# Mean and variance of every normalisation by `bn_aggr`, one per block of 128 tokens, in place of seven small operations

## The reference

```python
def _layernorm(x, axis=-1, eps=1e-05):
    m = jnp.mean(x, axis=axis, keepdims=True)
    v = jnp.var(x, axis=axis, keepdims=True)
    return (x - m) / jnp.sqrt(v + eps)
...
x = x + jnp.tanh(g_xattn[0]) * _L0_xattn_ref(_layernorm(x, axis=-1), ...)
x = x + jnp.tanh(g_ffn[0]) * _L0_ffn_ref(_layernorm(x, axis=-1), ...)
x = x + jnp.tanh(g_xattn[1]) * _L1_xattn_ref(_layernorm(x, axis=-1), ctx_1024, ctx_1024, ...)
x = x + jnp.tanh(g_ffn[1]) * _L1_ffn_ref(_layernorm(x, axis=-1), ...)
```

## Time and profile before

| what | value |
|---|---|
| median of 3 runs | 1592.85 us |
| lowest and highest run | 1590.7 and 1597.24 us |
| the profiled execution, from its first to its last instruction | 1595.5 us |
| DVE busy | 972.5 us, 61% of the span |
| PE busy | 1302.9 us, 82% |
| ACT busy | 1081.9 us, 68% |
| POOL busy | 528.5 us, 33% |
| mean granted TensorE clock | 0.920 of full speed |

### The profile page before, as it was taken

The page is one execution under the profiler, slowest core; times in us unless marked ns, Lnnn a source line. Parts: engine busy times, 40 slices in busy tenths (PEclk is TensorE's granted clock), DMA queues, the critical chain, the costliest instruction groups (busy, mean ns, idle before and its releaser), DMA issues.

```text
span 1595.5 us, 34655 instructions
## 1 busy us (share of the span) xinstructions
PE 1302.9 (82%) x11876; PEld 764.7 (48%) x11876; DVE 972.5 (61%) x2365; ACT 1081.9 (68%) x1781; POOL 528.5 (33%) x505
## 2 busy tenths in 40 slices
PE   6777776887588999998998899979997886888860
PEld 2212332343235554655475546554666575577650
DVE  7987558536743775388538854896468765223323
ACT  5998886867886799878987997769872431222220
POOL 1101121121453121425543445246425334503216
PEclk8978897988798999999999999999998997899995
DMA  7654402503132343454444554434346545579964
GB/s 225 223 188 123 105 1 67 137 4 83 69 90 73 87 121 86 103 157 140 140 113 120 148 143 113 128 102 152 100 126 192 144 132 135 164 191 236 252 174 119
DMA packets 234434, 207.60 MB, mean 130 GB/s; under 512 B 121945, under 2 KB 191137, under 8 KB 234273
## 3 DMA queue, kind: packets, MB, share of 16 engines
q1 hardware_dynamic: 210017, 160.29, 38.1%
q0 software_dynamic: 12288, 33.57, 6.6%
q10 hardware_dynamic: 11968, 11.54, 2.3%
HBM read 110.01 MB, written 70.16 MB: 113 GB/s over the span
## 4 chain that ended last, share of the span: by engine, by line
PE 48%; DVE 20%; ACT 18%; issue 7%; POOL 4%; DMA 1%; another core or an unknown queue 1%; SPq 0%; POOLq 0%; ACTq 0%; DVEq 0%
ACT tanh_tiles L1251 15%; PE psF L1020 8%; PE psE L866 6%; PE psE L868 5%; PE psE L867 5%; PE psY L866 3%; PE psY L867 2%; PE psY L868 2%; PE psF L872 2%; PE psF L866 2%; PE psF L868 2%; PE psF L867 2%; POOL work L852 2%; DVE stats L1428 2%; DVE xn L1454 1%
## 5 line engine op out<-in xcount | busy, mean ns | idle before, releaser
L1251 ACT ACTIVATE tanh_tiles<-feat,text_bias 128x512 f32<-128x512 f32 x1232 | 774.4, 713 | 74.1 <-DVE feat L1624 56.2
L1020 PE MATMUL psF<-tanh_tiles,wslide 128*32 128x512 f32 x2464 | 372.9, 662 | 61.7 <-ACT tanh_tiles L1251 60.5
L1653 DVE TENSOR_TENSOR tile<-tile,psE 128x512 f32<-128x512 f32 x128 | 87.5, 684 | 163.9 <-ACT tile L1278 80.6
L799 POOL TENSOR_TENSOR hid<-tile,hid 128x512 f16<-128x512 f32 x76 | 88.3, 1163 | 233.4 <-ACT hid L1270 231.8
L823 POOL DMA_INDIRECT xs_rows<-xs,slot_i x128 | 127.8, 998 | 111.7 <-PE psF L1020 40.3
L1270 ACT CAST hid<-tile 128x512 f16<-128x512 f32 x128 | 78.6, 614 | 125.5 <-DVE tile L1653 115.8
L866 PE MATMUL psY<-down,hid 128*128 128x256 f16 x512 | 143.3, 280 | 15.9 <-issue 10.1
L868 PE MATMUL psE<-xg,up_lo 128*128 128x128 f16 x768 | 146.8, 221 | 9.2 <-issue 9.1
L867 PE MATMUL psE<-xg,up_hi 128*128 128x128 f16 x768 | 147.3, 222 | 7.5 <-issue 7.5
L1278 ACT ACTIVATE tile<-psE 128x512 f32<-128x512 f32 x128 | 75.6, 591 | 114.7 <-remote 60.8
L866 PE MATMUL psE<-xg,up_hi 128*128 128x128 f16 x768 | 147.5, 222 | 6.7 <-issue 5.6
(11 more groups left out here) (306 smaller groups left out, 2883.9 us busy)
## 6 DMA issues: line engine op xcount, KB each, us to landing
down<-down_split SPq DMA_DIRECT2D x208, 256.0 KB
y_rows<-hid SPq DMA_DIRECT2D x52, 256.0 KB
xs_rows<-peakT SPq DMA_DIRECT2D x24, 512.0 KB, 6.4
y_rows<-tanh_tiles ACTq DMA_DIRECT2D x44, 256.0 KB
down_split<-hid SPq DMA_DIRECT2D x18, 256.0 KB, 3.2
xscan<-in_x SPq DMA_DIRECT2D x8, 512.0 KB, 5.1
x<-in_x SPq DMA_DIRECT2D x8, 512.0 KB, 5.3
w_lin<-w_split SPq DMA_DIRECT2D x15, 256.0 KB
```

The source lines that it names most:

```text
L799: pool.tensor_tensor(hid_lo[:, n], tile[:, v.n % 2], hid_hi[:, n], ALU.subtract).then_inc(glo_done, 1)
L1020: last = pe.matmul(psF[32 * j:32 * j + 32, RHO, :], wslide[:, c, 31 - g:63 - g], tanh_tiles[:, st.at(SETS, 2 * g + c) % HRING, j], start=g ...
L1251: act.activation(tanh_tiles[:, n % HRING, j], feat[:, c], ACT.Tanh, bias=text_bias[:, c, col:col + 1]).then_inc(h_ready, 1)
L1653: dve.tensor_tensor(tile[:, n], tile[:, n], psE[:, (2 * v.n + 1) % 3], ALU.mult).then_inc(g_done, 1)
```

## The change

The moments are finished by one `bn_aggr` for each block of 128 tokens, which turns the block's six columns into mean and variance and writes them to the block's column of `norm[:, 0]` and `norm[:, 1]`. The addition of EPS moves to the head of `inverse_root`, as an operation of its own, which writes `veps`. The three Newton iterations are written out in place of a loop of three; the instructions are the same.

```diff
             def moments(ch, src, norm):
 
-                mean = norm[:, 0]
                 for t in range(NT):
                     last = dve.bn_stats(stats[:, t, :], src[:, t, :])
                 ch.link(last)
-
-                dve.tensor_tensor(mean, stats[:, :, 1], stats[:, :, 4], ALU.add)
-                dve.tensor_tensor(dif[:, :], stats[:, :, 1], stats[:, :, 4], ALU.subtract)
-                ch.link(dve.tensor_tensor(veps[:, :], stats[:, :, 2], stats[:, :, 5], ALU.add))
-                dve.tensor_scalar(mean, mean, 0.5, None, ALU.mult)
-                dve.tensor_tensor(dif[:, :], dif[:, :], dif[:, :], ALU.mult)
-                ch.link(dve.tensor_scalar(veps[:, :], veps[:, :], 1.0 / D, EPS, ALU.mult, ALU.add))
-                ch.link(dve.scalar_tensor_tensor(out=veps[:, :], in0=dif[:, :], scalar=0.25, in1=veps[:, :],
-                                                 op0=ALU.mult, op1=ALU.add))
+                for t in range(NT):
+                    last = dve.bn_aggr(norm[:, :, t], stats[:, t, :])
+                ch.link(last)
 
             def inverse_root(ch, rstd):
 
+                ch.link(dve.tensor_scalar(veps[:, :], rstd, EPS, None, ALU.add))
                 ch.link(dve.tensor_scalar(rstd.bitcast(I32), veps[:, :].bitcast(I32), -0.5, 1597463007.0,
                                           ALU.mult, ALU.add))
-                for _ in range(3):
-                    ch.link(dve.tensor_tensor(nwt[:, :], rstd, rstd, ALU.mult))
...
+                ch.link(dve.tensor_tensor(nwt[:, :], rstd, rstd, ALU.mult))
...
```

More of the change, by code:

```diff
@@ new lines, in inverse_root @@
+                ch.link(dve.scalar_tensor_tensor(out=nwt[:, :], in0=nwt[:, :], scalar=-0.5, in1=veps[:, :],
+                                                 op0=ALU.mult, op1=ALU.mult))
+                ch.link(dve.scalar_tensor_tensor(out=rstd, in0=nwt[:, :], scalar=1.5, in1=rstd,
+                                                 op0=ALU.add, op1=ALU.mult))
+                ch.link(dve.tensor_tensor(nwt[:, :], rstd, rstd, ALU.mult))
+                ch.link(dve.scalar_tensor_tensor(out=nwt[:, :], in0=nwt[:, :], scalar=-0.5, in1=veps[:, :],
+                                                 op0=ALU.mult, op1=ALU.mult))
```

## The result

| | median us | runs | ratio to before (95% interval) |
|---|---|---|---|
| before | 1593.49 (1590.7 to 1597.24) | 5 | |
| changed | 1582.21 (1577.61 to 1584.59) | 5 | 0.9921 (0.9895 to 0.9948) |

The change makes the kernel 11.3 us faster, 0.8%. It was measured twice more beside the experiments, each time on a chip with its own level: 1602.99 to 1587.07, ratio 0.9892 (0.9862 to 0.9921), and 1556.52 to 1538.99, ratio 0.9881 (0.9863 to 0.9898). The intervals of the first and the third share only 0.9895 to 0.9898; the first gain is the smallest of the three.

The account below looks back on a forecast made before the run. No single engine bounds the chain (PE 48%, DVE 20%, ACT 18%); DVE counts at boundaries, standing behind POOL. 7.2 + 2.2 + 1.2 = 10.6 us off 1592.85 gives 1582.3, range 1573 to 1592.

Parts of the forecast that it names:

- The aggregation: In each norm, four bn_aggr replace seven DVE operations: 0.47 us in place of 0.89, never held by POOL.
- (a): Rival at the boundaries: POOL holds the aggregation as well; only 2.4 us gained, 1590 us; chance 0.10.
- (c): Rival in every norm: the aggregation is as long as bn_stats or longer; 1593 us, no change, or slower; chance 0.10.
- The head of the root: Start of inverse_root in each norm: the added linked tensor_scalar costs 0.20 us; no wait for POOL charged.
- A late boundary: Last four of six outer-step ends, where LN4 and scan norm meet: 1.8 us gained each, 7.2 us together.
- An early boundary: First two of six outer-step ends: 1.0 us gained at the first, 1.2 at the second, 2.2 us together.
- Six other norms: Norms on the chain away from the boundaries: each 0.2 us shorter, 1.2 us together.
- (b): Rival at the boundaries: half of the gain is absorbed where three engines meet; 1588 us; chance 0.20.
- (d): Rival at up to five boundaries: less PE idle avoids some clock drops; 5 us more gain, 1577 us; chance 0.13.
- Standing elsewhere: Two-input operations of the root, L1445 to L1448, could meet another POOL operation; no size, DVE's total standing decides.

Follow-up runs that it names:

- e5: The changed kernel itself, measured again on a second chip: 1587.07 us against 1602.99 for the kernel before, ratio 0.9892.
- e9: The changed kernel itself, measured again on a third chip: 1538.99 us against 1556.52 for the kernel before, ratio 0.9881.
- e11: Changed kernel with EPS addition and first root guess unlinked, and two Newton iterations in place of three: 1525.17 us, ratio to before 0.9801.
- e2: Changed kernel with the aggregation only in LN2, LN3 and LN4; the scan norms keep the seven operations: 1546.31 us, ratio to before 0.9933.
- e7: Kernel before, with POOL's two-input L807 (low half of xs) replaced by a fill with zeros: 1591.9 us, ratio to before 0.9923.
- e8: Changed kernel with POOL's L807 replaced by a fill with zeros: 1586.3 us, ratio to the kernel before 0.9894.

## Why the prediction was right

**The time.** Forecast 1582.3, 10.6 us less; measured 1582.21, 11.3 us less. The forecast stood against 1592.85, the median of three runs, and the 11.3 us against 1593.49, the median of five. The two later measurements give 15.9 and 17.5 us, so the closeness of the first is partly luck. The two traces are 16.6 us apart: 10.3 at the boundaries, where the sum had 9.4, and 6.3 elsewhere, where it had 1.2.

**The aggregation.** Forecast 0.47 us for four and no standing behind POOL; 0.42 and none in 128. Rivals (a) and (c) are out.

**The head of the root.** 0.20 us forecast, 688.68 to 688.87 in the trace.

**A late boundary.** 1.8 us each, 7.2 together. The traces show 2.17, 1.96, 1.86 and 2.83, together 8.8. ACT's cast holds `eT_lo`, then come the copy and the added link, as forecast. One releaser is another than forecast: the copy L1596 starts at 688.08 right behind `eT_lo`, with no wait for PE. Counted from the start of `bn_stats`, the casts end after 3.03 us, not after the 2.84 of the kernel before, and the copy starts after 3.85, where the forecast has 3.87 by PE's matmul; that the later casts and the missing wait come to the same time is luck. Of the excess of 1.6 us over the four, about 1 lies at the boundary whose clock before was lowest (0.87, a gain of 2.83), by the price read above.

**An early boundary.** Forecast 1.2 us for the second and 1.0 for the first; measured 1.67 and -0.19 (a loss). The first of the six is the term that was mis-sized. Its norm did get shorter, but what `feat` waits for there fell into a stretch at the 1.2 GHz level. First PE in the changed kernel, then in the kernel before, one of the twelve FEAT matmuls each:

```profile
246.40 0.63 PE L868 MATMUL psF<-xT_hi,w_scan 128*128 128x512 f16 x1
```

```profile
246.24 0.38 PE L868 MATMUL psF<-xT_hi,w_scan 128*128 128x512 f16 x1
```

In the kernel before the low stretch lay on the transposes ahead (L872, 1.88 us there, 1.09 in the changed kernel). The same changed kernel took 23.37 us here in e5 and 21.47 in e9, where the low stretch lay elsewhere; so the loss goes with the place of the low stretch, and the runs pin down no cost of the change itself.

**Six other norms, 1.2 us.** Not seen one by one. e11 fits the 18 norms that were taken, within wide bounds; e2 finds more than any count of norms explains, and that stays open.

**The rivals.** (b), half of the gain absorbed, is out at the late boundaries. (d), the clock, was given 0.13 as a case of its own, but it came on top of the forecast one: no late boundary drops its clock any more. Its price was put at 5 us, and 10.6 + 5 = 15.6 is close to the two later measurements (15.9 and 17.5), but the boundaries do not bear the price out: the drops there were worth some 1.1 us. The runs show that the late drops go away with the standing. Where the other 5 us or so of the later measurements come from is open; no run held the clock and changed the standing.

**Standing elsewhere.** The prediction left the decision to the total. What the norms' small operations took over 0.16 us each, added up over their groups by line, falls from 28.0 to 14.0 us. The moments had 15.5 of it and have none. The root had 12.5 and has 14.0, so 1.5 us of standing came back there. At LN4 a Newton operation meets L799 as before: L1443 at 529.96 for 1.15 us in the changed kernel. The head of the root, for which nothing was charged, has 3.2 us of the 14.0 where it had 0.5: L1435 takes up to 832 and L1436 up to 765 ns. DVE and POOL of the changed kernel:

```profile
138.98 0.76 DVE L1436 TENSOR_SCALAR norm<-veps 128x4 int32<-128x4 int32 x1
```

```profile
138.95 0.77 POOL L845 TENSOR_TENSOR xg<-work,xg 128x308 f16<-128x308 f32 x1 [0.26 <-DVE xg L1711]
```

In the kernel before it was the first Newton operation, L1445, that stood there, for 0.75 us.

## What to carry to other kernels

When a tiny DVE operation takes a microsecond in a trace, look at what POOL runs at that moment before counting operations: how many SBUF tiles the instruction reads can be worth more than how many instructions there are. Follow a saved stall to the next releaser of each engine that meets there; that gave 1.67 us where 1.70 was measured. A stall that leaves TensorE idle can also lower its clock afterwards; read the price of that from boundaries of the same kernel with and without the drop before adding it, here 0.1 us at most, or about 1 us for the deeper ones.

## What the runs showed of the hardware that was not expected

In e7 the zero fill, which reads nothing, ran from 236.74 to 237.69 us beside a norm of DVE. POOL, then DVE:

```profile
236.74 0.95 POOL L807 MEMSET xs<- 128x1024 f16 x1
```

```profile
237.01 0.16 DVE L1432 TENSOR_TENSOR dif<-stats 128x4 f32<-128x4 f32 x1
237.09 0.16 DVE L1433 TENSOR_TENSOR veps<-stats 128x4 f32<-128x4 f32 x1
237.28 0.44 DVE L1434 TENSOR_SCALAR scan_norm<-scan_norm 128x4 f32<-128x4 f32 x1
237.36 0.36 DVE L1435 TENSOR_TENSOR dif<-dif 128x4 f32<-128x4 f32 x1
```

The first two-input operations pass it unhindered, and the `tensor_scalar` with a single input ends at 237.72, with the fill; the two-input L1435 right behind it ends with it. POOL's operations on two tiles hold both kinds: the two-input ones at every boundary above, and a `tensor_scalar` at 138.98. The Trainium skill ("SBUF — State Buffer", section "Who interferes with whom") has both halves: two SBUF inputs contend only with a GpSimd operation that reads, and `tensor_scalar` in a two-port mode contends with any. The trace agrees on both. The aggregation passes in either case: beside L807 in the changed kernel, and beside the fill in e8, where none that overlaps it takes over 185 ns.

The mean granted clock of the whole execution also rises by 0.009 with the change, which was not expected. The late boundaries hold about half of the rise between the two first traces (0.920 to 0.928); the rest lies elsewhere, and no run shows that the idle taken out at the boundaries brings it.
